# A graph attention kernel whose node rows are stored twice, as K|V and as V|K, and whose V halves are stored in runs of 2 KB

## The chip, the cores and the metric

The kernel runs on one core of one Trainium2 chip. The metric is device time in microseconds (us) of one execution, the median of several. Data is float32 throughout, unless said otherwise.

## The reference

Two graph layers over 12,500 nodes of 256 numbers and 200,000 edges, sorted by destination. Only the first touches what is changed here:

```python
Q = (enh @ Wq + bq).reshape(N, H, D)      # enh = x + 0.1 * query_emb, H = 4, D = 64
K = (enh @ Wk + bk).reshape(N, H, D)
V = (enh @ Wv + bv).reshape(N, H, D)
mod_k  = K[src] + 0.2 * rel_w[edge_type][:, None, :]
scores = einsum('ehd,ehd->eh', Q[dst], mod_k) / D ** 0.5
w      = softmax of scores over the edges of each dst
agg    = segment_sum(w[:, :, None] * V[src], dst)
msgs   = where(deg > 0, agg, V)           # then @ Wo + bo, residual, two layernorms
```

The second layer gathers one 1040-byte row per edge, weighs it with a sigmoid and sums it by the other end.

## The kernel before, in words

The stages run one after the other, each in a block of its own in which every engine has its own program and the engines meet at semaphores.

- `project`: 98 blocks of 128 nodes. TensorE transposes x and multiplies it with Wk|Wv and Wq; VectorE adds the bias (L411) into one of four buffers `kv_out` of 128 x 512 numbers. SyncE (SP) loads x four blocks ahead (L264) and stores K|V, 2 KB a node, to `kv_rows` in DRAM (L287). VectorE may overwrite a `kv_out` buffer when the store of four blocks earlier has landed. VectorE also runs steps of a sort of the edges between the blocks.
- `edge_scores`: 416 groups of 4 x 128 edges. For each group GpSimd (POOL) issues four indirect gathers (L704), each of 128 rows of 2 KB from `kv_rows` into `rows`, a ring of `KV_RING` = 5 buffers `[128, 4, 512]`. A buffer holds K at numbers 0 to 255 and V at 256 to 511 of each of its four rows. It may be gathered into again when VectorE has finished the scores of the group five earlier and when the V halves of that group have landed in DRAM. SP stores those V halves to `v_edges` (L687): 512 pieces of 1 KB for a group, since K lies between them in SBUF. Ahead of it, SP issues the loads of edge codes, `spread` (L671), three groups ahead; ScalarE turns these into one-hot matrices, TensorE picks Q and relation rows with them, and VectorE makes the score of a group in three passes over K: add the relation (L801), multiply by Q (L805), reduce (L807). Steps of the edge sort's merge run on VectorE too, in groups 1 to 342.
- `softmax_numerators`: on chip only.
- `aggregate`: 416 groups again. SP loads the V halves of a group (L1071) into a ring of `DEEP` = 10 buffers `terms` of `[128, 4, 260]`, GpSimd multiplies them by the weights (L1082), TensorE sums them by node (L1157), VectorE adds the sums into the table of nodes (L1138).
- `update_nodes`, `attend` and `finish` follow. `update_nodes` reads V of each node from `kv_rows`.

`v_edges` is laid out by slot: row `(g*4 + k)*128 + p` holds the 256 numbers of edge slot k of group g in partition p, so the four rows of one partition lie 128 KB apart.

Of the kernel before, what the change touches and what calls it, by code (L numbers as in the profile page):

```python
# [8 lines left out]
ALU = mybir.AluOpType  # L9
ACT = mybir.ActivationFunctionType  # L10
AX = mybir.AxisListType

P = 128
N = 12500
E = 200000
D = 256
H = 4
# [154 lines left out]
def gnn_kernel(nc, x, src, dst, edge_type, query, wq, bq, wk, bk, wv, bv, rel_w, wo, bo, gamma, beta,  # L172
               w1, b1, w2, b2, wa1, ba1, wa2, ba2, out):
    with ExitStack() as ctx:
        def sb(name, shape, dt=fp32):
            return ctx.enter_context(nc.sbuf_tensor(name, shape, dt))

        def dram(name, shape, dt=fp32):
            return nc.dram_tensor(name, shape, dt, kind="Internal").ap()

        t = {"spent": []}
        t["kv_rows"] = dram("kv_rows", (N, 2 * D))
        t["v_edges"] = dram("v_edges", (S * P, D))
        t["xj_rows"] = dram("xj_rows", (N, XW))
        t["what_rows"] = dram("what_rows", (G, 2, IDS, P), u8)
        t["local0_in"] = dram("local0_in", (P, S))
        t["a1_rows"] = dram("a1_rows", (S, P))
        t["sorted_keys"] = dram("sorted_keys", (1 << LOGN,), i32)

        t["node_tab"] = sb("node_tab", [P, NB * AW])  # L190
        t["ident"] = sb("ident", [P, P])
        t["ident_h"] = sb("ident_h", [P, P], bf16)
        t["iota"] = sb("iota", [P, P])
        t["ones"] = sb("ones", [P, P])
        t["ones_h"] = sb("ones_h", [P, P], bf16)
        t["a1_tab"] = sb("a1_tab", [P, NB])

        t["x"], t["src"], t["dst"], t["edge_type"], t["out"] = x, src, dst, edge_type, out
        with ExitStack() as layer0:
            t["other0"] = layer0.enter_context(nc.sbuf_tensor("other0", [P, S], i32))  # L200
            t["places0"] = layer0.enter_context(nc.sbuf_tensor("places0", [P, S // 4], i32))
            t["score"] = layer0.enter_context(nc.sbuf_tensor("score", [P, S * H], fp32))
            t["keys"] = [layer0.enter_context(nc.sbuf_tensor(f"keys{u}", [P, F], i32)) for u in range(2)]
            t["two_signs"] = layer0.enter_context(nc.sbuf_tensor("two_signs", [P, 8], fp32))
            t["local0"] = t["keys"][0][:, 0:S].bitcast(fp32)
            project(nc, t, query, wq, bq, wk, bk, wv, bv)
            build_steps(nc, t, 0)
            edge_scores(nc, t, rel_w)
            softmax_numerators(nc, t)
            aggregate(nc, t)  # L210
        t["other1"] = sb("other1", [P, S], i32)
        t["local1"] = sb("local1", [P, S])
        t["places1"] = sb("places1", [P, S // 4], i32)
        t["block_hot"] = sb("block_hot", [P, S])
        t["step_id"], t["tile_base"] = sb("step_id", [P, S // 4], i32), sb("tile_base", [P, C])
        t["tile_end1"] = sb("tile_end1", [P, C, 2])
        with ExitStack() as middle:
            t["score"] = middle.enter_context(nc.sbuf_tensor("scratch", [P, 16 * D], fp32))
            build_steps(nc, t, 1)
            update_nodes(nc, t, wo, bo, gamma, beta, w1, b1, w2, b2, wa1, ba1, wa2, ba2)  # L220
        attend(nc, t)
        finish(nc, t)
# [3 lines left out]
def project(nc, t, query, wq, bq, wk, bk, wv, bv):  # L226
    x, tab, ident, ones = t["x"], t["node_tab"], t["ident"], t["ones"]
    with ExitStack() as ctx:
# [31 lines left out]
        @block.sync  # L260
        def _(sp):
            def load(b):
                r = rows_of(b)
                sp.dma_start(x_in[b % 4][0:r, :], x[b * P:b * P + r, :]).then_inc(x_loaded[b % 4], 16)  # L264

            load(0)
            with nc.allow_non_contiguous_dma(reason="256 numbers, once"):
                sp.dma_start(q_col[:, :], query.rearrange("(c p) -> p c", p=P)).then_inc(weights_in, 16)
            for n, w in ((1, wk), (2, wv), (0, wq)):
                sp.dma_start(w_qkv[:, :, n * D:(n + 1) * D], w.rearrange("(c p) n -> p c n", p=P)).then_inc(weights_in, 16)  # L270
            for b in range(1, 4):
                load(b)
            for n, a in enumerate((bq, bk, bv)):
                sp.dma_start(b_wide[:, n * D:(n + 1) * D], a.partition_broadcast(P)).then_inc(biases_in, 16)
            sp.wait_ge(pads_set, 1)
            for n, a in enumerate((t["src"], t["dst"])):
                sp.dma_start(keys[n][0:even_p, :], a[0:even_p * F].rearrange("(p f) -> p f", f=F)).then_inc(keys_in, 16)
                sp.dma_start(keys[n][even_p:full_p, :], a[even_p * F:full_p * F].rearrange("(p f) -> p f", f=F)).then_inc(keys_in, 16)
                sp.dma_start(keys[n][full_p:full_p + 1, 0:rest],
                             a[full_p * F:E].rearrange("(p f) -> p f", p=1)).then_inc(keys_in, 16)  # L280
            for b in range(NB):
                if b + 4 < NB:
                    sp.wait_ge(xt_ready, b + 1)
                    load(b + 4)
                r = rows_of(b)
                sp.wait_ge(kv_ready, b + 1)
                sp.dma_start(t["kv_rows"][b * P:b * P + r, :], kv_out[b % 4][0:r, :]).then_inc(kv_stored[b % 4], 16)  # L287
            for u in range(4):
                sp.wait_ge(kv_stored[u], 16 * len(range(u, NB, 4)))

        @block.gpsimd
        def _(pool):
# [62 lines left out]
        def _(dve):  # L355
# [51 lines left out]
            for b in range(NB):  # L407
                dve.wait_ge(kv_done, b + 1)
                if b >= 4:
                    dve.wait_ge(kv_stored[b % 4], 16 * (b // 4))  # L410
                dve.tensor_tensor(kv_out[b % 4][:, :], ps_kv[b % 2][:, :], b_wide[:, D:3 * D], ALU.add).then_inc(kv_ready, 1)  # L411
                if b >= 6:
                    next(sorting, None)
                dve.wait_ge(q_done, b + 1)
                dve.scalar_tensor_tensor(tab[:, b * AW:b * AW + D], ps_q[b % 2][:, :], float(DH) ** -0.5, b_wide[:, 0:D],
                                         ALU.mult, ALU.add).then_inc(q_kept, 1)
                if b >= 6 and b % 3:
                    next(sorting, None)
# [205 lines left out]
def edge_scores(nc, t, rel_w):  # L624

    with ExitStack() as ctx:
# [35 lines left out]
        def _(sp):  # L663
# [13 lines left out]
            for g in range(G):  # L677
# [5 lines left out]
                if g == MERGED_AT + 24:  # L683
                    sp.wait_ge(keys_out, 16)
                    sp.dma_start(t["local0"], t["local0_in"]).then_inc(local_in, 16)
                sp.wait_ge(rows_in[g % KV_RING], 16 * U * (g // KV_RING + 1))
                sp.dma_start(t["v_edges"][g * U * P:(g + 1) * U * P, :].rearrange("(k p) d -> p k d", p=P),  # L687
                             rows[g % KV_RING][:, :, D:2 * D]).then_inc(v_stored[g % KV_RING], 16)
            for u in range(KV_RING):
                sp.wait_ge(v_stored[u], 16 * len(range(u, G, KV_RING)))  # L690
            sp.wait_ge(local_in, 16)
# [2 lines left out]
        def _(pool):  # L694
# [4 lines left out]
            for g in range(G):  # L699
                if g >= KV_RING:  # L700
                    pool.wait_ge(scored, g - KV_RING + 1)
                    pool.wait_ge(v_stored[g % KV_RING], 16 * (g // KV_RING))
                for k in range(U):
                    pool.indirect_dma_start(out=rows[g % KV_RING][:, k, :], out_offset=None, in_=t["kv_rows"],  # L704
                                            in_offset=bass.IndirectOffsetOnAxis(ap=t["other0"][:, g * U + k:g * U + k + 1], axis=0))\
                        .then_inc(rows_in[g % KV_RING], 16)

# [29 lines left out]
        def _(dve):  # L737
# [56 lines left out]

            merging = merge()
            for g in range(G):
                key = rows[g % KV_RING][:, :, 0:D]
                by_head = key.rearrange("p k (h d) -> p k h d", h=H)
                dve.wait_ge(rel_copied, g + 1)
                dve.wait_ge(rows_in[g % KV_RING], 16 * U * (g // KV_RING + 1))  # L800
                dve.tensor_tensor(by_head, by_head, rel[g % 2][:, :, :].unsqueeze(2).broadcast_to([P, U, H, DH]), ALU.add)\  # L801
                    .then_inc(rows_used, 1)
                dve.wait_ge(rows_used, g + 1)
                dve.wait_ge(picked, g + 1)
                dve.tensor_tensor(key, key, ps_q[g % PICKS][:, :, :], ALU.mult).then_inc(picked_used, 1)  # L805
                dve.wait_ge(picked_used, g + 1)
                dve.tensor_reduce(t["score"][:, g * U * H:(g + 1) * U * H].rearrange("p (k h) -> p k h", h=H), by_head, AX.X, ALU.add)\  # L807
                    .then_inc(scored, 1)
                if 1 <= g <= MERGED_AT:
                    next(merging)  # L810
# [232 lines left out]
def aggregate(nc, t):  # L1043
    with ExitStack() as ctx:
# [22 lines left out]
        def _(sp):  # L1067
            for g in range(G):
                if g >= DEEP:
                    sp.wait_ge(summed, g - DEEP + 1)  # L1070
                sp.dma_start(terms[g % DEEP][:, :, 0:D],  # L1071
                             t["v_edges"][g * U * P:(g + 1) * U * P, :].rearrange("(k p) d -> p k d", p=P)).then_inc(rows_in[g % DEEP], 16)

        @block.gpsimd
        def _(pool):
# [634 lines left out]
```

## Time and profile before

| | |
|---|---|
| runs | 6409.14 us, median of 3 (6407.86 to 6410.38) |
| the profiled execution's own time | 6408.69 us |
| its span, first to last instruction | 6406.9 us |
| TensorE / VectorE / ScalarE / GpSimd busy | 68% / 69% / 41% / 67% of the span |
| mean DMA rate | 209 GB/s, 1336.78 MB in all |
| edge scores | about 345 to 2858 us |
| aggregate | about 2992 to 3875 us |

How to read it. A DMA engine is one of 16 that move data, whichever queue asked for it. The profile names the queues: q0 carries what GpSimd issues (the gathers), q1 what SP issues, q10 what ScalarE issues. "Share of 16 engines" is the summed time of a queue's packets over 16 times the stretch, so share x stretch x 16 is engine time, and dividing by the bytes gives what a piece costs. An SP instruction of a DMA ends when its descriptors have been handed over, not when its data has landed; "to landing" is from issue to the last byte's semaphore. Idle time before an instruction is put down to whatever released it.

### The profile page before, as it was taken

To read this page: it belongs to the slowest core of one execution; us is meant where nothing else is said; L and a number is where in the kernel's file an instruction comes from. 1 tells how busy PE (TensorE), PEld (TensorE's weight loads), DVE (VectorE), ACT (ScalarE), POOL (GpSimd) and SP (SyncE) were. 2 spreads that over 40 slices of the span, in tenths; PEclk is the share of its full clock that TensorE was granted. 3 is DMA by queue.
4 is the path that set the end of the run, shared out by engine and by line. 5 is a ranking of instruction groups with operands and counts; after the bars stand their busy time and mean duration, and the time that the engine had idled before them with its cause. 6 is when DMAs were issued, how large, how long until landed. Compare 5 with 4: busy or idle time off the path is not lost. (4 is left out here: it accounts for less than half of the span.)

```text
span 6406.9 us, 69655 instructions
## 1 busy us (share of the span) xinstructions
PE 4357.6 (68%) x14703; PEld 2942.1 (46%) x14703; DVE 4425.0 (69%) x9217; ACT 2622.0 (41%) x6438; POOL 4315.8 (67%) x4007
## 2 busy tenths in 40 slices
PE   9856655565555666554999997996666666666663
PEld 5544444444444444442666664443443343333332
DVE  8857777777777776568888887994555555555557
ACT  2133333333333333334888884772222222222223
POOL 0057677777777766653988884556777777777772
PEclk9977777777777777776999998997777777777775
DMA  4378888888888888872877873335666666666664
GB/s 150 124 238 280 277 279 278 277 280 280 278 279 279 278 278 282 278 230 90 249 246 247 247 247 100 102 94 162 161 161 162 162 161 162 162 162 161 161 162 140
DMA packets 863748, 1336.78 MB, mean 209 GB/s; under 512 B 88283, under 2 KB 640467, under 8 KB 863017
## 3 DMA queue, kind: packets, MB, share of 16 engines
q0 software_dynamic: 208288, 644.62, 35.2%
q1 hardware_dynamic: 588137, 572.24, 27.9%
q10 hardware_dynamic: 66914, 115.46, 6.0%
q8 instruction: 135, 2.21, 0.2%
q14 instruction: 274, 2.24, 0.1%
HBM read 1059.09 MB, written 272.90 MB: 208 GB/s over the span
## 5 line engine op out<-in xcount | busy, mean ns | idle before, releaser
L704 POOL DMA_INDIRECT s_rows<-kv_rows,other x1664 | 1783.9, 1072 | 717.5 <-issue 495.4
L1507 POOL DMA_INDIRECT t_rows<-xj_rows,other x1564 | 1494.7, 956 | 492.6 <-issue 476.2
L1609 PE MATMUL ps_xsum<-t_rows,t_att 128*128 x3328 | 1263.2, 535 | 712.8 <-DVE t_att L1562 712.5
L1609 PEld LDWEIGHTS ps_xsum<-t_rows,t_att 128*128 128x128 f32 x3328 | 770.2, 258 | 1206.1 <-issue 911.8
L1562 DVE SCALAR_TENSOR_TENSOR t_att<-iota,local,t_att 128x128 f32<-128x128 f32 x1664 | 579.7, 349 | 950.4 <-ACT t_att L1541 948.0
L834 PE MATMUL ps_q<-node_tab,hot 128*128 x3328 | 1161.0, 512 | 0.0
L1541 ACT ACTIVATE t_att<-t_att,t_rows 128x128 f32<-128x128 f32 x1664 | 531.2, 389 | 1429.9 <-SPq L1494 1417.4
L828 PE MATMUL ps_small<-rel,hot 128*128 128x128 f32 x1664 | 397.1, 377 | 1014.0 <-ACT hot L722 1014.0
L718 ACT ACTIVATE apart<-spread,minus_p 128x768 uint8<-128x768 uint8 x416 | 388.8, 935 | 1574.7 <-DMA spread<-what_rows 1574.7
L801 DVE TENSOR_TENSOR s_rows<-s_rows,rel 128x1024 f32<-128x1024 f32 x416 | 510.4, 1227 | 718.0 <-ACT rel L734 717.7
L834 PEld LDWEIGHTS ps_q<-node_tab,hot 128*128 128x128 f32 x3328 | 856.4, 270 | 154.6
L1157 PE MATMUL ps_sum<-a_terms,a_hot 128*128 128x260 f32 x3328 | 830.6, 393 | 72.4 <-DVE node_tab L1138 48.4
L1082 POOL TENSOR_TENSOR a_terms<-a_terms,score 128x1024 f32<-128x1024 f32 x416 | 782.0, 1903 | 104.6 <-DMA a_terms<-v_edges 90.9
L828 PEld LDWEIGHTS ps_small<-rel,hot 128*128 128x128 f32 x1664 | 298.0, 253 | 1199.7 <-ACT hot L722 1199.0
L1138 DVE TENSOR_TENSOR node_tab<-node_tab,ps_sum 128x260 f32 x1664 | 705.3, 424 | 156.1 <-PE ps_sum L1157 53.6
L1157 PEld LDWEIGHTS ps_sum<-a_terms,a_hot 128*128 128x128 f32 x3328 | 600.1, 190 | 302.9 <-issue 214.9
L1576 DVE TENSOR_TENSOR node_tab<-node_tab,ps_xsum 128x256 f32 x1664 | 691.1, 415 | 2.1 <-DVE node_tab L1576 0.6
L805 DVE TENSOR_TENSOR s_rows<-s_rows,ps_q 128x1024 f32<-128x1024 f32 x416 | 507.8, 1221 | 14.3
L807 DVE TENSOR_REDUCE score<-s_rows 128x16 f32<-128x1024 f32 x416 | 507.5, 1220 | 14.2
L1091 ACT ACTIVATE a_far<-iota,keys 128x128 bf16<-128x128 f32 x1456 | 469.3, 389 | 4.7 <-PEq L851 4.7
L722 ACT ACTIVATE hot<-apart,ones 128x768 f32<-128x768 uint8 x416 | 388.8, 935 | 13.6
L1104 ACT ACTIVATE a_hot<-a_far,ones 128x512 f32<-128x512 bf16 (+1 forms) x416 | 278.1, 669 | 142.1 <-PE ps_sum L1157 136.7
(226 smaller groups left out, 3794.0 us busy)
## 6 DMA issues: line engine op xcount, KB each, us to landing
v_edges<-s_rows SPq DMA_DIRECT2D x416, 512.0 KB, 13.4
a_terms<-v_edges SPq DMA_DIRECT2D x416, 512.0 KB, 4.3
t_att<-a_rows ACTq DMA_DIRECT2D x416, 256.0 KB, 3.6
spread<-what_rows SPq DMA_DIRECT2D x416, 96.0 KB
s_rows<-kv_rows,other POOLq DMA_INDIRECT x1664, 5.3
t_rows<-xj_rows,other POOLq DMA_INDIRECT x1564, 3.3
kv_rows<-kv_out SPq DMA_DIRECT2D x97, 256.0 KB, 2.0
xj_rows<-n_hx SPq DMA_DIRECT2D x97, 130.0 KB, 2.3
```

What stands on the lines that cost most here:

```text
L704: pool.indirect_dma_start(out=rows[g % KV_RING][:, k, :], out_offset=None, in_=t["kv_rows"], in_offset=bass.IndirectOffsetOnAxis(ap=t["oth ...
L801: dve.tensor_tensor(by_head, by_head, rel[g % 2][:, :, :].unsqueeze(2).broadcast_to([P, U, H, DH]), ALU.add)\
L828: last = nc.tensor.matmul(ps_rel[g % 2][:, 2 * j:2 * j + 2, :], hot[g % HOTS][:, U + j, :], rel_02[:, :, :], start=True, stop=True)
L834: last = nc.tensor.matmul(ps_q[g % PICKS][:, k, :], hot[g % HOTS][:, k, :], q[k], start=True, stop=True)
L1082: nc.gpsimd.tensor_tensor(by_head, by_head, weight.unsqueeze(3).broadcast_to([P, U, H, DH]), ALU.mult).then_inc(weighed, 1)
L1138: dve.tensor_tensor(acc, acc, ps_sum[g % 2][:, k, 0:AW], ALU.add).then_inc(added, 1)
L1157: last = nc.tensor.matmul(ps_sum[g % 2][:, k, 0:AW], hot[g % 4][:, k, :], terms[g % DEEP][:, k, :], start=True, stop=True)
L1507: pool.indirect_dma_start(out=rows[:, at:at + XW], out_offset=None, in_=t["xj_rows"], in_offset=bass.IndirectOffsetOnAxis(ap=t["other1"][: ...
L1541: last = nc.scalar.activation(att[g % ATT_RING][:, k, :], att[g % ATT_RING][:, k, :], ACT.Sigmoid, bias=a2[k])
L1562: dve.scalar_tensor_tensor(w, t["iota"][:, :], t["local1"][:, g * U + k:g * U + k + 1], w, ALU.is_equal, ALU.mult)\
L1576: dve.tensor_tensor(acc, acc, ps_sum[g % 4][:, k, :], ALU.add).then_inc(added, 1)
L1609: nc.tensor.matmul(ps_sum[g % 4][:, k, :], att[g % ATT_RING][:, k, :], xj[k], start=True, stop=True)\
```

## The change

`project` stores every block three times over: K|V into `kv_rows` as before, and the two halves crosswise into a second table `vk_rows`, as V|K, in pieces of 1 KB. The semaphore counts that follow are tripled. `edge_scores` gathers rows k = 0 and 2 of a group from `kv_rows` and rows k = 1 and 3 from `vk_rows`, so that in a pair of rows the order in SBUF is K, V, V, K: the two V halves are adjacent, 2 KB. They are stored as one run, and `v_edges` is laid out as `[group, partition, k, 256]`, so that a partition's four V halves are 4 KB in a row in DRAM. VectorE's three passes address K with a step of 768 numbers inside a pair and 1024 between pairs. The load in `aggregate` reads the new layout; its destination keeps rows of 256 numbers at a pitch of 260.

```diff
-        t["v_edges"] = dram("v_edges", (S * P, D))
+        t["vk_rows"] = dram("vk_rows", (N, 2 * D))
+        t["v_edges"] = dram("v_edges", (G, P, U, D))
...
                 sp.dma_start(t["kv_rows"][b * P:b * P + r, :], kv_out[b % 4][0:r, :]).then_inc(kv_stored[b % 4], 16)
+                for half in range(2):
+                    sp.dma_start(t["vk_rows"][b * P:b * P + r, half * D:(half + 1) * D],
+                                 kv_out[b % 4][0:r, (1 - half) * D:(2 - half) * D]).then_inc(kv_stored[b % 4], 16)
             for u in range(4):
-                sp.wait_ge(kv_stored[u], 16 * len(range(u, NB, 4)))
+                sp.wait_ge(kv_stored[u], 3 * 16 * len(range(u, NB, 4)))
...
                 if b >= 4:
-                    dve.wait_ge(kv_stored[b % 4], 16 * (b // 4))
+                    dve.wait_ge(kv_stored[b % 4], 3 * 16 * (b // 4))
...
                 sp.wait_ge(rows_in[g % KV_RING], 16 * U * (g // KV_RING + 1))
-                sp.dma_start(t["v_edges"][g * U * P:(g + 1) * U * P, :].rearrange("(k p) d -> p k d", p=P),
-                             rows[g % KV_RING][:, :, D:2 * D]).then_inc(v_stored[g % KV_RING], 16)
+                sp.dma_start(t["v_edges"][g, :, :, :].rearrange("p (pair two) d -> p pair (two d)", two=2),
+                             rows[g % KV_RING][:, :, :].rearrange("p (pair two) d -> p pair (two d)", two=2)[:, :, D:3 * D])\
+                    .then_inc(v_stored[g % KV_RING], 16)
...
-                    pool.indirect_dma_start(out=rows[g % KV_RING][:, k, :], out_offset=None, in_=t["kv_rows"],
+                    pool.indirect_dma_start(out=rows[g % KV_RING][:, k, :], out_offset=None, in_=t["vk_rows"] if k % 2 else t["kv_rows"],
...
-                key = rows[g % KV_RING][:, :, 0:D]
-                by_head = key.rearrange("p k (h d) -> p k h d", h=H)
+                key = rows[g % KV_RING][:, :, :].rearrange("p (pair two) (half d) -> p pair (two half) d", two=2, half=2)[:, :, 0:4:3, :]
+                by_head = key.rearrange("p pair two (h d) -> p pair two h d", h=H)
...
                 sp.dma_start(terms[g % DEEP][:, :, 0:D],
-                             t["v_edges"][g * U * P:(g + 1) * U * P, :].rearrange("(k p) d -> p k d", p=P)).then_inc(rows_in[g % DEEP], 16)
+                             t["v_edges"][g, :, :, :]).then_inc(rows_in[g % DEEP], 16)
```

SP in `project`, blocks 1 to 3, before. `kv_out1` is the buffer of block 1, `x_in2` that of a later block's x.

```order
L287 DMA kv_rows<-kv_out1 128x512
L264 DMA x_in2<-in_x 128x256
L287 DMA kv_rows<-kv_out2 128x512
L264 DMA x_in3<-in_x 128x256
L287 DMA kv_rows<-kv_out3 128x512
```

The same place of the changed kernel:

```order
L288 DMA kv_rows<-kv_out1 128x512
L290 DMA vk_rows<-kv_out1 128x256 x2
L265 DMA x_in2<-in_x 128x256
L288 DMA kv_rows<-kv_out2 128x512
L290 DMA vk_rows<-kv_out2 128x256 x2
L265 DMA x_in3<-in_x 128x256
```

Two more stores stand between the store of a block and the next load of x.

SP in `edge_scores`, from the fourth load of edge codes on, before:

```order
L671 DMA spread3<-what_rows 128x1x768
L687 DMA v_edges<-s_rows0 128x4x256
L671 DMA spread0<-what_rows 128x1x768
L687 DMA v_edges<-s_rows1 128x4x256
L671 DMA spread1<-what_rows 128x1x768
```

And now:

```order
L675 DMA spread3<-what_rows 128x1x768
L691 DMA v_edges<-s_rows0 256x1x512
L675 DMA spread0<-what_rows 128x1x768
L691 DMA v_edges<-s_rows1 256x1x512
L675 DMA spread1<-what_rows 128x1x768
```

Nothing moved; each store is of 256 runs of 512 numbers where it was of 512 runs of 256.

## Rows read from the trace of the kernel before

**Rows 1.** Windows: us, busy PE, PEld, DVE, ACT, POOL, clock, DMA share, GB/s.

```profile
0.00:200.00 200.00, 192.00 (x676) 115.38 (x677) 173.93 (x243) 44.78 (x141) 5.76 (x15) 1.00 0.47 148
345.00:2858.00 2513.00, 1509.30 (x5216) 1150.54 (x5216) 1778.62 (x1563) 916.26 (x1361) 1784.21 (x1666) 0.76 0.87 278
2990.00:3870.00 880.00, 812.67 (x3256) 587.17 (x3256) 726.92 (x1834) 738.71 (x2263) 778.03 (x414) 0.99 0.81 249
```

**Rows 2.** Source line 704, GpSimd's gathers: shortest/median/longest ns, and idle time before them.

```profile
L704 POOL DMA_INDIRECT s_rows<-kv_rows,other x1664: 951/957/2009, 345.8 to 2845.8; - x185
...
  issue: 495.4, 1505
  DMA v_edges<-s_rows: 221.5, 157
```

**Rows 3.** Waits between 345 and 2858 us: in total, times, longest.

```profile
ACT apart L718 <- DMA spread<-what_rows: 1574.7, 416, 7.4
...
DVE s_rows L801 <- ACT rel L734: 717.7, 393, 26.3
```

**Rows 4.** Source line 801, the first of VectorE's three passes over a group's K.

```profile
L801 DVE TENSOR_TENSOR s_rows<-s_rows,rel x416: 1211/1226/1296, 359.2 to 2856.6; 128x1024 f32<-128x1024 f32 x139
```

**Rows 5.** Timeline of SP's queue, four of the rows between 1505 and 1517 us.

```profile
1505.54 3.60 SPq L687 DMA_DIRECT2D v_edges<-s_rows  x1
1509.18 1.98 SPq L671 DMA_DIRECT2D spread<-what_rows  x1
1511.21 4.13 SPq L687 DMA_DIRECT2D v_edges<-s_rows  x1
1515.39 1.68 SPq L671 DMA_DIRECT2D spread<-what_rows  x1
```

**Rows 6.** DMA view, 345 to 2858 us: queue, kind: packets, MB, share of 16 engines.

```profile
q0 software_dynamic: 133120, 436.31, 56.7%
q1 hardware_dynamic: 274176, 260.96, 30.6%
...
v_edges<-s_rows SPq DMA_DIRECT2D x416, 512.0 KB, 13.4
```

**Rows 7.** DMA view, 1483.4 to 1485.4 us in 40 slices: engines busy in tenths, rate.

```profile
DMA  3760495389559068224110400210012001111111
GB/s 102 261 164 0 184 507 246 164 348 753 246 246 671 16 277 343 113 97 179 82 82 0 179 0 0 97 82 0 15 46 97 31 15 46 46 46 46 46 46 46
```

**Rows 8.** Timeline of GpSimd and SP's queue around that stretch.

```profile
1481.72 3.73 SPq L687 DMA_DIRECT2D v_edges<-s_rows  x1
1483.71 1.74 POOL L704 DMA_INDIRECT s_rows<-kv_rows,other  x1 [1.48 <-DMA v_edges<-s_rows]
```

**Rows 9.** DMA view, 6380 to 6400 us, q1: only stores of 1 KB pieces, `out<-f_y`.

```profile
q1 hardware_dynamic: 1872, 1.70, 24.4%
```

**Rows 10.** DMA view, 333 to 335.5 us: one store in 128 pieces of 6656 bytes.

```profile
q1 hardware_dynamic: 144, 0.85, 84.1%
```

**Rows 11.** DMA view, 30 to 270 us, projection: stores of 2 KB, loads of 1 KB.

```profile
q1 hardware_dynamic: 24591, 33.53, 43.6%
```

**Rows 12.** DMA view, 3000 to 3870 us, aggregate: only loads of 1 KB pieces.

```profile
q1 hardware_dynamic: 217012, 215.51, 80.2%
```

**Rows 13.** Source line 287, the stores of K|V, and 264, the loads of x.

```profile
L287 SPq DMA_DIRECT2D kv_rows<-kv_out x98: 320/327/353, 12.9 to 285.7; - x98
...
DMA to landing us min/median/max: 2.0/2.0/7.5
...
L264 SPq DMA_DIRECT2D x_in<-in_x x98: 332/432/596, 0.7 to 272.9; - x98
```

**Rows 14.** Waits between 2990 and 3875 us, the first line SP's queue from 3100 to 3800.

```profile
SPq L1071 <- PE ps_sum L1157: 577.4, 329, 2.2
...
PE ps_sum L1157 <- DVE node_tab L1138: 47.5, 209, 0.6
...
PE ps_sum L1157 <- POOL a_terms L1082: 14.4, 1, 14.4
```

More of the change, by code:

```diff
@@ L796, in _ @@
             for g in range(G):
-                key = rows[g % KV_RING][:, :, 0:D]
-                by_head = key.rearrange("p k (h d) -> p k h d", h=H)
+                key = rows[g % KV_RING][:, :, :].rearrange("p (pair two) (half d) -> p pair (two half) d", two=2, half=2)[:, :, 0:4:3, :]
+                by_head = key.rearrange("p pair two (h d) -> p pair two h d", h=H)
                 dve.wait_ge(rel_copied, g + 1)
                 dve.wait_ge(rows_in[g % KV_RING], 16 * U * (g // KV_RING + 1))
-                dve.tensor_tensor(by_head, by_head, rel[g % 2][:, :, :].unsqueeze(2).broadcast_to([P, U, H, DH]), ALU.add)\
+                dve.tensor_tensor(by_head, by_head, rel[g % 2][:, :, :].rearrange("p (pair two) d -> p pair two d", two=2)
+                                  .unsqueeze(3).broadcast_to([P, U // 2, 2, H, DH]), ALU.add)\
                     .then_inc(rows_used, 1)
@@ L804, in _ @@
                 dve.wait_ge(picked, g + 1)
-                dve.tensor_tensor(key, key, ps_q[g % PICKS][:, :, :], ALU.mult).then_inc(picked_used, 1)
+                dve.tensor_tensor(key, key, ps_q[g % PICKS][:, :, :].rearrange("p (pair two) d -> p pair two d", two=2), ALU.mult).then_inc(picked_used, 1)
                 dve.wait_ge(picked_used, g + 1)
-                dve.tensor_reduce(t["score"][:, g * U * H:(g + 1) * U * H].rearrange("p (k h) -> p k h", h=H), by_head, AX.X, ALU.add)\
+                dve.tensor_reduce(t["score"][:, g * U * H:(g + 1) * U * H].rearrange("p (pair two h) -> p pair two h", two=2, h=H), by_head, AX.X, ALU.add)\
                     .then_inc(scored, 1)
```

## The prediction, made before the changed kernel was run

> **What bounds the kernel now.** I read the windows by stage first. Edge scores take 2513 of the 6406.9 us and no engine is full there: TensorE 60%, VectorE 71%, GpSimd 71%; the DMA engines are busy 87% of it at 278 GB/s [rows 1]. So the question is what 416 groups of 6.04 us wait for. GpSimd issues the gathers, four a group, and all its time can be told: 1784 us busy, 495 us in the fixed pause before a gather, 222 us waiting for a V store to free its buffer, in sum 6.01 us a group [rows 1, 2]. If each gather took the median 957 ns and nothing were waited for, a group would take 4 x 0.957 + 495.4/416 = 5.02 us: a floor, a good 1 us below. VectorE waits 718 us for relation rows, those come after ScalarE, and ScalarE waits 1575 us for the load of codes [rows 3]. VectorE's three passes at 1.23 us [rows 4] are not the limit.
>
> The load of codes and the V stores are both SP's, and SP's queue has no room: store 3.60, codes 1.98, store 4.13, codes 1.68 us, back to back, about 5.7 us of each 6.0 [rows 5]. These are not costs of an issue: the stores of K|V in the projection are handed over in 327 ns [rows 13]. SP is held back because the rings it fills are full, and a store takes 13.4 us to land [rows 6]. Who empties them? Look at one stretch of 2 us: its last seven slices show a tenth of the engines at 46 GB/s [rows 7]. One engine storing 1 KB pieces moves 1.70 MB in 0.244 x 20 x 16 = 78.1 us, 21.8 GB/s [rows 9], so 46 GB/s is two engines at full speed while fourteen rest. In that time SP sits in a store for 3.73 us and GpSimd waits 1.48 us for a V store [rows 8]. My reading: **a couple of DMA engines lag behind the others with V stores and set the pace**; the mean of 87% hides them (which engines these are, no view tells).
>
> **The change, part by part.** All sums are against the profiled execution, 6408.69 us (1.8 us outside its span), 0.45 us under the median of 6409.14.
>
> *V stores, 256 runs of 2 KB for 512 of 1 KB.* A piece costs a fixed part and a part by bytes. In 1 KB stores the engine time per KB is 78.1 us / 1660 = 47.0 ns [rows 9]. In 6656-byte stores it is 0.841 x 2.5 x 16 / 128 = 263 ns a piece [rows 10]. The slope is 216/5632 ns a byte, 39.3 ns a KB, which leaves 7.8 ns fixed (unrounded) and makes a 2 KB piece 86.3 ns against 94.1 for two of 1 KB. Per group each engine has 16 pairs: 16 x 7.8 = 0.124 us. It counts in full, since the engines that set the pace have no gap to lose it in: 416 x 0.124 = **52 us less**. The bounds: the most a piece's fixed part could be is what 1 KB loads in the aggregate show, 0.802 x 870 x 16 / 215.51 MB = 53.0 ns a KB, less the same slope: 13.7 ns, 0.22 us a group, 91 us less [rows 12]. The other end is the nearest row with 2 KB stores, the projection: 0.436 x 240 x 16 us for 33.53 MB is 20.0 GB/s an engine, 102.3 ns for 2 KB, so 16 x (102.3 - 94.1) = 0.13 us a group, 55 us more [rows 11]. I take 7.8 ns: rows 9 and 10 are stores alone, rows 11 mix them with loads of 1 KB, in short transfers of eight pieces an engine.
>
> The Trainium skill ("DMA: Bandwidth & Descriptors", Specifications) has 512 B as the smallest transfer for line rate. By that nothing would be gained between 1 KB and 2 KB, and this term would be 0 instead of 52 us less; it is a rival below.
>
> *Gathers from two tables.* As many rows of 2 KB, of indices as random as before: 416 x 4 instructions at 957 ns [rows 2]. A second address on GpSimd: 0. Where the rows lie in DRAM changes, and I see no row that prices it.
>
> *VectorE's steps of 768 and 1024.* As many elements; the pass that reads PSUM and the reduction too. Cover: the 718 us, 1.7 us a group, that it waits for relation rows [rows 3]. If an extra dimension cost 0.1 us in each of three passes, 0.3 us a group would still be hidden. If that cover were gone it would be 125 us, but a wait for scores is not in GpSimd's list worth a line, only the V store is [rows 2].
>
> *Two more stores a block in the projection.* SP issues 2 x 0.33 us more a block [rows 13]; with its load of x (0.43) and the first store that is 1.42 us of a block's 2.8 (272.8 us from the first to the last of 98). DMA: 256 pieces more at 47.0 ns, 12.0 us of engine time over 16 x 2.8, share from 0.47 to about 0.74. TensorE covers it, busy 192 of 200 us [rows 1]. The next load of x stands behind the two stores, 0.65 us later, but is needed more than two blocks on. The buffer's reuse waits for three semaphores' worth, four blocks, 11 us, for 2.0 us landings: the tripled wait holds up nothing. Uncovered are the last block's stores, 0.65 us of issue and their landing, and the first ones, which run beside the bulk loads (landings up to 7.5 us) [rows 13]. I take **2 us more**, bound 0 to 10.
>
> *The load in the aggregate.* DRAM is read in 4 KB runs, but SBUF is still written in 1 KB pieces, at a pitch of 1040 B. The stage is 81% DMA [rows 1], yet TensorE waited for GpSimd once, 14.4 us at the start, and SP waits 577 of 700 us for TensorE before it may load [rows 14]. A ring of ten groups is cover for any load that keeps pace. 0, whichever way it goes; a stage that waits for TensorE and VectorE gets nothing from faster loads.
>
> Sum: 6408.69 - 52 + 2 = 6358.7, with the 0.45 us to the median **6359 us**, 0.8% less. By its own bounds 6318 to 6474.
>
> **The rivals.** *Room in the rings.* What holds SP may be the number of descriptors in flight rather than the engines' work. The store then has half of them, SP runs ahead, buffers come free earlier and the gaps of the fourteen others fill. The two queues also share an engine: a turn of SP's queue now brings twice the bytes. For it: SP's 5.7 us, the gaps in rows 7, a floor of 5.02 us. Against it: two engines at full speed need time for their bytes, whoever waits. If it took away just GpSimd's wait for V stores it would give 221.5 us: 6408.7 - 221.5 + 2 = **6189**. All the way to the floor would be 6.04 - 5.02 = 1.02 us a group, 424 us, 5987; that needs DMA engines 100% busy at today's prices and I leave it out.
> The skill ("DMA: Bandwidth & Descriptors", Queues, rings and completion order) says an engine round-robins between queue rows packet by packet, which is what this rival needs; that V stores take 13.4 us to land fits.
>
> *Bytes alone.* If an engine's time is its bytes, or the lag comes from the gathers' reads, which cost 0.567 x 2513 x 16 / 212,992 = 107 ns a row of 2 KB, twice the store's rate in ns [rows 6], shorter lists of stores change nothing: only the projection's 2 us are left, **6411**.
>
> *Slower.* The 2 KB piece costs 102 ns as in rows 11, since it holds the path to DRAM longer and the gathers' reads wait behind it. It turns from gain to loss where a 2 KB store passes 94.1 ns of engine time, or, at my 86.3, where a gathered row passes 107 + 4 = 111 ns (32 rows an engine a group against 0.124 us). Price 55 + 2 more: **6466**.
>
> **How the numbers follow.** The forecast holds 0.42 (6320 to 6390 of its own), room in the rings 0.19, bytes alone 0.17, slower 0.22. About 0.2%, 13 us, is what a measurement of this kernel tells from no change. Forecast and rings are both faster: 0.61. Bytes alone is the same, with a little of the slow case's edge: 0.18. Slower 0.21. The signs of most of the chance agree, but the range must reach both sides: from 6185, just under the rings' 6189, to 6455, which leaves out the far part of the slow case and of the rings. The likeliest case's own range, 6320 to 6390, stands beside it.
>
> **What would show it.** Forecast: in edge scores q1 has about 106,000 packets fewer (416 x 256), its share falls from 30.6% to about 29%, a gathered row stays near 107 ns, a group takes 5.91 us, SP's store and codes still fill its time and GpSimd still waits for V stores. Rings: SP's store falls far under 3.6 us, landing well under 13.4, GpSimd's 221 us wait is gone. Bytes: fewer packets, same share, same 2513 us. Slower: a 2 KB store near 102 ns of engine time, or a gathered row over 111 ns. In every case aggregate stays within a few us of 880 and the projection ends at most some us later. I am wrong altogether if VectorE's passes go well over 1.23 us, if the aggregate moves by more than 10 us, or if the gathers from two tables have another price than from one.

## The result, and the profile after

The changed kernel takes **6379.69 us** (median of 6 runs, 6377.41 to 6381.79), the kernel before 6409.76 us in the same comparison (6 runs). The ratio is 0.9954, 95% interval 0.9944 to 0.9964: 30 us less, or 0.46%. Forecast were 6359 us, 50 us less, in a range of 6185 to 6455. The sign and the stage were right, and so was the kind of mechanism, two DMA engines that lag; the size was three fifths of what was said.

The profiled execution took 6381.05 us, its span 6379.2. Windows of the same columns as [rows 1]: projection, edge scores, aggregate.

```profile
0.00:200.00 200.00, 190.63 (x675) 114.59 (x676) 173.18 (x241) 44.16 (x139) 5.76 (x15) 1.00 0.74 234
345.00:2831.00 2486.00, 1517.35 (x5216) 1154.44 (x5216) 1780.41 (x1564) 916.52 (x1361) 1784.49 (x1666) 0.75 0.87 281
2963.00:3841.00 878.00, 811.98 (x3253) 586.73 (x3254) 724.42 (x1828) 738.08 (x2261) 776.84 (x414) 0.99 0.80 249
```

The source lines of the gathers and of the last of VectorE's passes: shortest/median/longest ns, first and last start.

```profile
L709 POOL DMA_INDIRECT s_rows<-kv_rows,other x832: 951/957/2004, 347.5 to 2815.9; - x167
L709 POOL DMA_INDIRECT s_rows<-vk_rows,other x832: 951/957/2017, 348.9 to 2817.2; - x167
...
  issue: 485.8, 1507
  DMA v_edges<-s_rows: 194.5, 154
...
L813 DVE TENSOR_REDUCE score<-s_rows x416: 1219/1220/1221, 364.6 to 2830.3; 128x16 f32<-128x1024 f32 x139
```

The row of before that answers to the last one:

```profile
L807 DVE TENSOR_REDUCE score<-s_rows x416: 1219/1220/1221, 361.7 to 2859.1; 128x16 f32<-128x1024 f32 x139
```

I measure the stage from its first gather to the start of its last reduction. Before it is 2859.1 - 345.8 = 2513.3 us [rows 2], now 2830.3 - 347.5 = 2482.8: **30.5 us less, 0.073 us a group**. It starts 1.7 us later, the projection's price, and what follows costs 1.1 us more (the span is 27.7 us shorter, the last reduction 28.8 earlier). These three make up the 27.7 us.

Waits in edge scores, from 350 to 2840 us, and the first pass, for [rows 3, 4]: nothing there has turned.

```profile
ACT apart L723 <- DMA spread<-what_rows: 1542.9, 416, 7.0
...
DVE s_rows L806 <- ACT rel L739: 687.3, 398, 27.5
```

```profile
L806 DVE TENSOR_TENSOR s_rows<-s_rows,rel x416: 1209/1226/1299, 362.1 to 2827.8; 128x1024 f32<-128x1024 f32 x139
```

SP's queue, for [rows 5], and the DMA view from 350 to 2840 us, for [rows 6]:

```profile
1497.74 4.48 SPq L691 DMA_DIRECT2D v_edges<-s_rows  x1
1502.27 0.58 SPq L675 DMA_DIRECT2D spread<-what_rows  x1
1502.89 5.16 SPq L691 DMA_DIRECT2D v_edges<-s_rows  x1
1508.09 1.30 SPq L675 DMA_DIRECT2D spread<-what_rows  x1
```

```profile
q0 software_dynamic: 133089, 436.19, 58.1%
q1 hardware_dynamic: 167520, 260.93, 28.5%
...
v_edges<-s_rows SPq DMA_DIRECT2D x416, 512.0 KB, 14.4
```

Over the whole stage q1 has 106,496 packets fewer, 256 a group, and yet SP is held as long as before, 5.1 and 6.5 us for store and codes together in these rows; its stores even longer, 4.5 us in the median against 3.8, the loads of codes shorter. Stores land in 14.4 us, not 13.4. A gathered row takes 0.581 x 2490 x 16 / 212,992 = 108.7 ns of engine time, against 107.

The projection's stores, for [rows 13]:

```profile
L290 SPq DMA_DIRECT2D vk_rows<-kv_out x196: 387/448/683, 14.9 to 287.2; - x196
```

### The profile page after: what moved, and what is told of

Same layout as the page of the kernel before. It is cut to its first block and busy times, and to the rows that moved or that the text cites. A ratio compares the mean times of both kernels' runs of the same rounds, so it can differ in the third digit from the quotient of the medians.

```text
span 6379.2 us, 69851 instructions
## 1 busy us (share of the span) xinstructions
PE 4348.0 (68%) x14703; PEld 2925.8 (46%) x14703; DVE 4423.7 (69%) x9217; ACT 2622.2 (41%) x6438; POOL 4317.9 (68%) x4007
## 5 line engine op out<-in xcount | busy, mean ns | idle before, releaser
L1615 PE MATMUL ps_xsum<-t_rows,t_att 128*128 x3328 | 1247.0, 528 | 729.2 <-DVE t_att L1568 728.6
L1615 PEld LDWEIGHTS ps_xsum<-t_rows,t_att 128*128 128x128 f32 x3328 | 751.1, 253 | 1225.5 <-issue 924.2
L709 POOL DMA_INDIRECT s_rows<-kv_rows,other x832 | 906.0, 1089 | 419.2 <-issue 225.0
L709 POOL DMA_INDIRECT s_rows<-vk_rows,other x832 | 878.2, 1056 | 267.8 <-issue 260.8
L806 DVE TENSOR_TENSOR s_rows<-s_rows,rel 128x1024 f32<-128x1024 f32 x416 | 510.2, 1226 | 687.5 <-ACT rel L739 687.3
## 6 DMA issues: line engine op xcount, KB each, us to landing
v_edges<-s_rows SPq DMA_DIRECT2D x416, 512.0 KB, 14.4
```

Source lines behind the costliest of these rows:

```text
L806: dve.tensor_tensor(by_head, by_head, rel[g % 2][:, :, :].rearrange("p (pair two) d -> p pair two d", two=2) .unsqueeze(3).broadcast_to([P ...
L1615: nc.tensor.matmul(ps_sum[g % 4][:, k, :], att[g % ATT_RING][:, k, :], xj[k], start=True, stop=True)\
```

## The experiments

My theory was that the two DMA engines that lag set the pace, so that what such an engine has to do for a group counts in full. The rivals: room in the rings (descriptors), bytes alone, the place of the pieces in DRAM, the two tables. Stage lengths below are all taken as above, from the first gather to the start of the last reduction. Comparisons with the kernel before are by ratio, with a 95% interval.

**e1_layout: the new layout alone.**

```diff
-        t["v_edges"] = dram("v_edges", (S * P, D))
+        t["v_edges"] = dram("v_edges", (G, P, U, D))
-                sp.dma_start(t["v_edges"][g * U * P:(g + 1) * U * P, :].rearrange("(k p) d -> p k d", p=P),
+                sp.dma_start(t["v_edges"][g, :, :, :],
                              rows[g % KV_RING][:, :, D:2 * D]).then_inc(v_stored[g % KV_RING], 16)
```

> The kernel before with the new layout of v_edges alone (group, partition, k): one table, V stores in 512 pieces of 1 KB as before. Theory (a store costs by its pieces and bytes on the DMA engines that set the pace): no piece has changed, 6410 us, within 5. Rival (the gain comes from where the pieces lie in DRAM, four to a 4 KB run, or from the aggregate's loads of 4 KB runs): up to all of the 30 us, 6380.

Ratio 1.0002 (0.9993 to 1.0012). No gain comes from where the pieces lie, nor from the aggregate's loads of 4 KB runs.

**e2_tables: two tables, both K|V.**

```diff
+                for half in range(2):
+                    sp.dma_start(t["vk_rows"][b * P:b * P + r, half * D:(half + 1) * D],
+                                 kv_out[b % 4][0:r, half * D:(half + 1) * D]).then_inc(kv_stored[b % 4], 16)
...
-                    pool.indirect_dma_start(out=rows[g % KV_RING][:, k, :], out_offset=None, in_=t["kv_rows"],
+                    pool.indirect_dma_start(out=rows[g % KV_RING][:, k, :], out_offset=None, in_=t["vk_rows"] if k % 2 else t["kv_rows"],
```

> The kernel before with a second table that holds K|V too, stored in two pieces of 1 KB a row, and rows k = 1 and 3 gathered from it; V stores and their layout as before. Theory: only the projection's 2 us, 6412. Rival (two tables make the gathers dearer, which is what took 22 of the forecast's 52 us): a gathered row costs 1 to 2 ns more engine time, 32 rows an engine and group, 13 to 27 us, 6425 to 6440.

Ratio 1.0003 (0.9993 to 1.0013), edge scores 2512.9 us, starting 1.7 us later. Two tables cost nothing that these runs can tell from zero (0.1%, 6 us), and the missing 22 us of the forecast do not lie there.

**e3_half_kb and e4_half_bytes: the pieces doubled; the bytes halved.**

```diff
+                for half in range(2):
+                    sp.dma_start(t["v_edges"][half, g * U * P:(g + 1) * U * P, :].rearrange("(k p) d -> p k d", p=P),
+                                 rows[g % KV_RING][:, :, D + half * D // 2:D + (half + 1) * D // 2]).then_inc(v_stored[g % KV_RING], 16)
```

> The kernel before with V stored in 1024 pieces of 512 bytes a group, by two DMAs, and loaded so in the aggregate. Theory (pieces): 32 more pieces an engine and group at 7.8 ns, 0.25 us a group, edge scores 104 us longer. Rival (the rings' room in descriptors is what holds SP): an engine's descriptors a group go from about 42 to 74, three quarters more, and edge scores grow by far more than 104 us, 300 and over. Bytes alone: edge scores stay at 2514 us.

```diff
-                             rows[g % KV_RING][:, :, D:2 * D]).then_inc(v_stored[g % KV_RING], 16)
+                             rows[g % KV_RING][:, :, D:D + D // 2]).then_inc(v_stored[g % KV_RING], 16)
```

> The kernel before with only the first half of each V row stored, 512 pieces of 512 bytes a group; the aggregate loads that half twice, so the sums of the other half are of wrong numbers. As many pieces, half the bytes. Theory (engine time sets the pace): a 1 KB piece costs 47.0 ns, a 512-byte piece 27.4 by the same fit; 32 x 19.6 = 0.63 us a group, 5.41 us instead of 6.04, edge scores 261 us shorter, still above the gathers' floor of 5.02. Rival (room in the rings, by descriptors): as many descriptors, edge scores stay near 2514 us.

e4 leaves half of each V row unstored. The last reductions and first gathers of the two, e3 first:

```profile
L705 POOL DMA_INDIRECT s_rows<-kv_rows,other x1664: 951/957/1998, 345.4 to 2910.6; - x185
...
L808 DVE TENSOR_REDUCE score<-s_rows x416: 1219/1220/1221, 362.6 to 2923.9; 128x16 f32<-128x1024 f32 x139
```

```profile
L704 POOL DMA_INDIRECT s_rows<-kv_rows,other x1664: 952/957/1999, 345.4 to 2683.5; - x185
...
L687 SPq DMA_DIRECT2D v_edges<-s_rows x416: 354/363/3703, 356.4 to 2689.4; - x139
...
L807 DVE TENSOR_REDUCE score<-s_rows x416: 1219/1220/1221, 361.3 to 2692.0; 128x16 f32<-128x1024 f32 x139
...
  DMA v_edges<-s_rows: 29.3, 96
```

e3: ratio 1.0102 (1.0085 to 1.0119), stage 2578.5 us, 65.2 more, 0.157 us a group: 4.9 ns for each of an engine's 32 added pieces, where 7.8 were forecast (one more DMA a group is in it too). The rival of the rings wanted 300 us and has fallen; bytes alone wanted none and has fallen too. e4: ratio 0.9748 (0.9732 to 0.9764), the last reduction starts at 2692.0 us, the stage has 2346.6, 167 us less where 261 were forecast. The descriptors were as many as before, and yet SP's store is handed over in 363 ns in the median, not 3.8 us, and GpSimd's wait for V stores is down from 222 to 29 us. So e4 has reached another limit, GpSimd's gathers, at 5.64 us a group and not at the floor of 5.02, and its 167 us say only that half the bytes were worth at least that much.

**e5_ring4: four gather buffers.**

```diff
-KV_RING = 5
+KV_RING = 4
```

> The changed kernel with four gather buffers instead of five. Theory (the DMA engines' work sets the pace; buffers are waited for because their stores are queued): edge scores lose little, under 40 us. Rival (a group's own chain of gather, landing, store and landing sets the pace, over the number of buffers): the chain of 5 x 5.97 = 29.9 us over 4 is 7.5 us a group, edge scores 620 us longer.

Median 6381.34 us (4 runs) against the changed kernel's 6379.69; stage 2481.2 us. A fifth buffer buys nothing. GpSimd waits as long for V stores as with five, 196 us against 194.5, and SP's store is held 2.7 us in the median instead of 4.5. I read this as a queue behind a saturated engine, which fewer buffers only make shorter.

**e6_split and e9_unload: V stores moved between engines.**

```diff
+                for lo, hi in ((0, 120), (120, 128)):
+                    sp.dma_start(t["v_edges"][g, lo:hi, :, :].rearrange("p (pair two) d -> p pair (two d)", two=2),
+                                 rows[g % KV_RING][lo:hi, :, :].rearrange("p (pair two) d -> p pair (two d)", two=2)[:, :, D:3 * D])\
+                        .then_inc(v_stored[g % KV_RING], 16)
```

> The changed kernel with each group's V store as two DMAs, of 120 and of 8 partitions. By the Trainium skill (DMA: Bandwidth & Descriptors, Why a DMA increments its semaphore by 16) the first runs on the lowest 15 engines and the second on the lowest 8, so the last engine gets no V store, engines 0 to 7 get 18 pieces and 8 to 14 get 16 as before. Theory (two engines lag, one the last of the sixteen, the other among the lower eight): no gain, since the other now has 2 pieces more, up to 0.1 us a group, 0 to 43 us longer; where the stores drain after a gap the rate is 23 GB/s, one engine, and no longer 46. Rivals: one engine alone paces and it is the last: over 200 us shorter; the last is none of the two: 46 GB/s in the gaps as before, 0 to 43 us longer.

```diff
-                for lo, hi in ((0, 120), (120, 128)):
+                for lo, hi in ((0, 96), (96, 117), (117, 124), (124, 128)):
```

> The changed kernel with each group's V store as four DMAs, of 96, 21, 7 and 4 partitions, which by the skill's rule run on 16, 7, 7 and 4 of the lowest engines: engines 7 to 15 get 12 pieces of 2 KB a group instead of 16, engines 0 to 3 get 22 and 4 to 6 get 20. Theory (the two lagging engines are both among 7 to 15; six tenths of an engine's store time shows in the group's time, as the runs with 512-byte pieces and half the bytes gave): 4 x 86.7 x 0.6 = 0.21 us a group, 87 us shorter. Rival (a lagging engine is among the lower seven, or they all lag in turn): 6 x 86.7 x 0.6 = 0.31 us, up to 130 us longer.

```profile
L814 DVE TENSOR_REDUCE score<-s_rows x416: 1219/1220/1221, 363.3 to 2898.5; 128x16 f32<-128x1024 f32 x139
```

```profile
L814 DVE TENSOR_REDUCE score<-s_rows x416: 1219/1220/1222, 364.8 to 3036.2; 128x16 f32<-128x1024 f32 x139
```

The Trainium skill ("DMA: Bandwidth & Descriptors", Why a DMA increments its semaphore by 16 and not by 1) says that a DMA issued by SP runs on the lowest-numbered k engines. The engine numbers below hold if that rule does; no view names an engine.

e6 (first row, first gather at 346.2): median 6448.12 us, stage 2552.3, 69.5 us longer than the changed kernel's, 0.167 us a group for 2 pieces more on the lower eight. e9 (second row, first gather at 347.5): median 6588.29 us, stage 2688.7, 205.9 us longer, 0.495 us for 6 pieces more on engines 0 to 3. Both give 83 ns a piece of 2 KB. But in both every 2 pieces come with one more DMA a group, so they could as well be the price of a DMA, 0.167 and 0.165 us, and e3, with one more DMA too, cost 0.157.

The spacing of packets tells the two apart. There are stretches in which only two engines still have work and all packets are of one size; then stretch x 2 / packets is the whole price of a packet. Three of them: the kernel before from 2455.65 to 2456.75 us and from 2578.25 to 2578.546, and e5 from 2369.63 to 2370.03:

```profile
DMA packets 67, 0.05 MB, mean 47 GB/s; under 512 B 0, under 2 KB 67, under 8 KB 67
q1 hardware_dynamic: 67, 0.05, 13.7%
```

```profile
DMA packets 14, 0.01 MB, mean 48 GB/s; under 512 B 0, under 2 KB 14, under 8 KB 14
q1 hardware_dynamic: 14, 0.01, 13.6%
```

```profile
DMA packets 10, 0.02 MB, mean 51 GB/s; under 512 B 0, under 2 KB 0, under 8 KB 10
q1 hardware_dynamic: 10, 0.02, 13.1%
```

Two of 16 engines are a share of 12.5%; what is over it is the overlap of records, see below. Rate x stretch / packets gives 772, 1015 and 2040 bytes: codes, V stores of 1 KB, V stores of 2 KB. The prices are 1.10 x 2 / 67 = 32.8 ns, 0.296 x 2 / 14 = 42.3 ns and 0.40 x 2 / 10 = 80.0 ns. So two pieces of 2 KB are 0.160 of e6's 0.167 us, six are 0.480 of e9's 0.495, and 5 to 7 ns are left for each added DMA. The price of a whole piece counts in full.

My theory about *where* the lagging engines are fell: taking a quarter of the stores off engines 7 to 15 helped nothing. The stage paid for six pieces in e9, which engines 0 to 3 got more, and not for the four of engines 4 to 6; so the lagging ones are among the lowest, as far as the rule holds. In e6 unloading the last engine gave nothing either. In both there are still two that lag, with the same packets of 768 bytes: e6 from 2489.05 to 2489.75 us, e9 from 2049.6 to 2050.1.

```profile
DMA packets 42, 0.03 MB, mean 46 GB/s; under 512 B 0, under 2 KB 42, under 8 KB 42
```

```profile
DMA packets 31, 0.02 MB, mean 48 GB/s; under 512 B 0, under 2 KB 31, under 8 KB 31
```

**e8_same_rows: one set of rows gathered again and again.**

```diff
-                                            in_offset=bass.IndirectOffsetOnAxis(ap=t["other0"][:, g * U + k:g * U + k + 1], axis=0))\
+                                            in_offset=bass.IndirectOffsetOnAxis(ap=t["other0"][:, 0:1], axis=0))\
```

> The kernel before with every gather using the first column of indices, the same 128 rows of 2 KB each time, so all scores and sums are of wrong rows. Bytes, pieces and instructions are as before. Question: why a gathered row costs 107 ns where a 2 KB store costs 86. If reading random rows of DRAM makes it, a row falls to 86 ns or under, an engine's work a group by 32 x 21 = 0.67 us and more, and edge scores shorten by 250 to 424 us (the gathers' floor of 5.02 us). If the way gathers are described and started makes it, nothing changes, 2514 us.

Ratio 0.9999 (0.999 to 1.0009), stage 2513.8 us. Random rows cost nothing over repeated ones, so DRAM's rows are not why a gathered row takes 107 ns (the gathers' share of the engines is 56.8% against 56.7%).

**e10_codes_before and e11_codes_after: the codes on all engines.** What is left on two engines when the others rest? Packets of 768 bytes, the load of codes, in the stretch of before above. Its source is `[2, 64 copies, 768]`, so its outermost size is 2.

```diff
-                sp.dma_start(spreads[g % SPREAD][:, :, :].rearrange("p n e -> p (n e)"),
-                             t["what_rows"][g, :, :, :].rearrange("h n e -> h (n e)").unsqueeze(1).broadcast_to([2, R, IDS * P]))\
-                    .then_inc(spread_in[g % SPREAD], 16)
+                for half in range(2):
+                    sp.dma_start(spreads[g % SPREAD][half * R:(half + 1) * R, :, :].rearrange("p n e -> p (n e)"),
+                                 t["what_rows"][g, half, :, :].rearrange("n e -> (n e)").partition_broadcast(R))\
+                        .then_inc(spread_in[g % SPREAD], 16)
```

> The kernel before with each load of edge codes (L671, 128 pieces of 768 bytes) as two DMAs of 64 partitions, one for each half, instead of one DMA whose source has the outermost size 2. Theory (new, from the runs that moved V stores between engines: the two lagging engines are among the lowest, and they lag because the load of codes runs on two engines only): with the codes spread over 16 engines an engine's queue work a group is 32 x 47.9 + 8 x 36 ns = 1.8 us of q1 and about 3.4 us of gathers, 5.2 us, beside the gathers' floor of 5.02: 5.1 to 5.35 us a group, edge scores 290 to 390 us shorter, and SP's store falls to a few tenths of a us. Rival (the codes already run on all engines, and two engines are slow by nature): no change, or 10 us longer for the second DMA.

> The changed kernel with the load of edge codes as two DMAs of 64 partitions. Theory: near the gathers' floor of 5.02 us a group, 2090 to 2180 us of edge scores, 300 to 390 us shorter than the changed kernel; against the kernel before with the same codes the changed V stores are worth between nothing (if the floor holds both) and the 30 us they are worth now. Rival (two engines slow by nature): no change, 6380 us.

Edge scores of e10, by window, q1 from 345 to 2661 us, SP's queue, and its gathers:

```profile
345.00:2661.00 2316.00, 1447.44 (x5216) 1104.39 (x5216) 1771.07 (x1564) 917.18 (x1361) 1800.42 (x1666) 0.78 0.95 302
```

```profile
q1 hardware_dynamic: 286648, 261.00, 33.4%
```

```profile
1506.67 0.37 SPq L688 DMA_DIRECT2D v_edges<-s_rows  x1
1507.08 1.88 SPq L672 DMA_DIRECT2D spread<-what_rows  x2
1510.21 0.37 SPq L688 DMA_DIRECT2D v_edges<-s_rows  x1
```

```profile
L705 POOL DMA_INDIRECT s_rows<-kv_rows,other x1664: 952/957/2012, 345.6 to 2651.7; - x185
...
  issue: 464.6, 1524
  DMA v_edges<-s_rows: 42.7, 140
```

```profile
L808 DVE TENSOR_REDUCE score<-s_rows x416: 1219/1220/1221, 359.0 to 2660.7; 128x16 f32<-128x1024 f32 x139
```

This is the cause, and the version that beats both kernels: **e10, 6208.59 us, ratio 0.9684 (0.967 to 0.9697)**, 200 us less for a few lines. The mean DMA share goes from 87% to 95%, SP's store from 3.8 to 0.37 us, GpSimd's wait for V stores from 222 to 43 us, the stage to 2315.1 us, 198 less. It is the same number of bytes and pieces, in one DMA more.

e11, the same on the changed kernel, has 6214.38 us, ratio 0.9695 (0.9682 to 0.9708): the interval overlaps e10's, and the two can't be told apart. Once the lowest engines no longer lag, GpSimd's gathers are the limit, and what the change saves is hidden.

The limit that is left was sized wrongly by me: 5.1 to 5.35 us a group expected, 2315.1/416 = 5.57 measured. GpSimd's own rows add up to it, 1800 + 465 + 43 = 2308 us. Its median gather is still 957 ns, the mean 1082: some take up to 2.0 us to issue. The same mean stood in the kernel before: 1784 us for 1664 gathers [rows 1, 2] are 1072 ns each, so the floor was 4 x 1.072 + 495.4/416 = 5.48 us and not 5.02. The median had hidden the long ones. Why some take so long, I have not tried; it stays open.

## Why the prediction was right, and where it was off

*What bounds the kernel.* Right as to the kind: two engines busy while the others rest, SP held by them, buffers waited for. It was shown by e4 (bytes off, SP free), e5 (fewer buffers, same time), e6 and e9 (full price of the added pieces) and e10. That it is full rings by which SP is held is argued, not shown. What I did not ask is *why* two engines lag. "With V stores" was a misreading of the stretch: 46 GB/s in a slice of 50 ns is 2304 bytes, three packets of 768, so it was the codes that two engines still moved [rows 7]; 15 and 31 are one and two such packets. Rows 5 held a hint too: a load of codes, 96 KB, held SP for 2 us in the same queue as a 512 KB store. e10 named it.

*The V stores.* The step that was off is the fixed part of a piece, 7.8 ns. Measured are 0.073 us a group for 16 pieces fewer, 4.6 ns each, and 4.9 ns each for 32 more (e3). Then 16 x 4.6 x 416 = 31 us, not 52. "It counts in full" was right, as the added 2 KB pieces at 80 ns show. The spacings agree: 2 x 42.3 - 80.0 = 4.6 ns. I had taken the fixed part from durations in packet records, and those overlap their neighbours. In the same stretches the records last 0.136 x 0.296 x 16 / 14 = 46.0 ns at 1 KB and 0.131 x 0.40 x 16 / 10 = 83.8 ns at 2 KB, 3.7 and 3.8 ns more than the spacing (3.2 for the codes). So the fixed part comes out of the records as 2 x 46.0 - 83.8 = 8.2 ns and out of the spacing as 4.6: that is what 7.8 had too much. At full stage length the records mislead in the same way: q1's time an engine falls by 0.306 x 2513 - 0.285 x 2490 = 59 us, twice what the stage gained.

The prices lie on one line, 37.7 ns a KB and 4.6 fixed: 80.0 at 2 KB, 42.3 at 1 KB, and 32.9 at 768 bytes, where the spacing gave 32.8. e3 adds (42.3 + 4.9)/2 = 23.6 at 512 B, where the line has 23.5. As an estimate from them the lagging engines had, before, 64 pieces of codes at 32.8 ns, 2.1 us, and 32 stores, 1.35 us, which leaves 2.6 of 6.04 us for 32 gathered rows, 81 ns each. By the records a gathered row has 107 ns in the mean of all engines; what makes the difference is not shown.

*Gathers, VectorE, projection, aggregate.* As forecast: two tables at no measurable cost (e2), passes at 1226 ns as before, the stage's start 1.7 us later where 2 was said, the aggregate within 1 us:

```profile
PE ps_sum L1163 <- DVE node_tab L1144: 46.9, 210, 0.6
PE ps_sum L1163 <- POOL a_terms L1088: 14.4, 1, 14.4
```

TensorE waits for VectorE and not for GpSimd, as in [rows 14].

*The rivals.* Room in the rings: fallen in e3. Its observable, a store handed over in far less than 3.6 us, came out the other way, 4.5 us in the median. Its far end, 5987, rested on the floor of 5.02 us, which is 5.48 with the mean gather. Bytes alone: fallen, in e3 and in the result. Slower at 102 ns a piece: fallen, it is 80. The 512 B that the Trainium skill ("DMA: Bandwidth & Descriptors", Specifications) has as the smallest transfer for line rate is not where the gain ends here: from 512 B to 1 KB to 2 KB a KB costs 47.2, 42.3 and 40.0 ns.

## What to carry to other kernels

A mean DMA share of 87% may be two engines at 100%: when an SP queue is held and the slices of the DMA line drop to a tenth at a rate of one or two engines, divide the bytes of such a stretch by its packets. The size names what is left on those engines. If its outermost size is small (2 here), split it, before making anything else smaller. Merging runs of 1 KB into 2 KB was worth some 5 ns of engine time a pair, and nothing once the two engines no longer set the pace (e11 against e10). Fixed costs are better taken from the spacing of packets, or from two runs that differ in piece count, than from packet durations. And a floor is made of means, not of medians.

## What the runs showed of the hardware that I had not expected

- A load of 96 KB whose source has an outermost size of 2 cost 198 us of a 2513 us stage; as two loads of 64 partitions those 198 us were gone.
- On a busy engine a packet of 768 bytes, 1 KB or 2 KB starts 32.8, 42.3 or 80.0 ns after the one before it, while its record lasts 36.0, 46.0 or 83.8 ns.
- Gathering one and the same 128 rows each time was no faster than random rows of a 25 MB table (ratio 0.9999).
- With `v_edges` laid out by partition its transfers take longer to hand over, though it costs no time here: the shortest V store 513 ns against 359, the aggregate's load 518 against 360 in the median. e1, whose layout alone is new, has it too (512 and 518); the aggregate's loads land in 4.8 us instead of 4.3. Row of the changed kernel, of e1 and of before:

```profile
L1077 SPq DMA_DIRECT2D a_terms<-v_edges x416: 517/518/1700, 2963.2 to 3839.9; - x139
```

```profile
L1071 SPq DMA_DIRECT2D a_terms<-v_edges x416: 517/518/1875, 2994.8 to 3872.1; - x139
```

```profile
L1071 SPq DMA_DIRECT2D a_terms<-v_edges x416: 359/360/1614, 2992.0 to 3867.8; - x139
```
